# A latent-attention block: value-output parts loaded piece by piece, a query product over 128 rows, low parts of rotated weights on GpSimd

## The reference

```python
q_lat = rmsnorm(x @ q_a_w, q_a_norm_w)                       # 192 wide
q = (q_lat @ q_b_w).reshape(b, s, H, QKD).transpose(0, 2, 1, 3)
q_nope, q_pe = (q[..., :NOPE], q[..., NOPE:])                # 128, 64 (rotated)
kv = (rmsnorm(kv_lat, kv_a_norm_w) @ kv_b_w)...              # k_nope, v from 64
scores = (einsum(q_nope, k_nope) + einsum(q_pe, k_pe)) * QKD ** (-0.5)
idx_scores = einsum('bqn,bnqk->bqk', iw, relu(einsum('bqnd,bkd->bnqk', iq, ik)))
_, topk_idx = jax.lax.top_k(where(causal, idx_scores, -inf), 128)
attn = softmax(where(topk_mask & causal, scores, -inf))
out = einsum('bhqk,bhkd->bqhd', attn, v).reshape(b, s, H * VD) @ o_w
```

## Time and profile before

| | |
|---|---|
| median of 3 runs | 976.77 us (971.97 to 983.13) |
| profiled execution | 975.21 us, its span 973.4 us |
| TensorE busy | 841.5 us, 86% of the span |
| VectorE busy | 700.1 us, 72% |
| ScalarE busy | 597.6 us, 61% |
| GpSimd busy | 517.8 us, 53% |
| mean granted TensorE clock | 0.958 |
| DMA engines' mean busy share in queue 1 | 41.1% |

### The profile page before, as it was taken

The page is one execution under the profiler, slowest core; times in us unless marked ns, Lnnn a source line. Parts: engine busy times, 40 slices in busy tenths (PEclk is TensorE's granted clock), DMA queues, the critical chain, the costliest instruction groups (busy, mean ns, idle before and its releaser), DMA issues.

```text
span 973.4 us, 20180 instructions
## 1 busy us (share of the span) xinstructions
PE 841.5 (86%) x7496; PEld 503.0 (52%) x7496; DVE 700.1 (72%) x1589; ACT 597.6 (61%) x1324; POOL 517.8 (53%) x407
## 2 busy tenths in 40 slices
PE   5979989877775989888998998999999999929998
PEld 2535544443343555555555665666666666614443
DVE  5366677899999999999997777678777777710100
ACT  3657789875564878788877666567666666610000
POOL 2093378755442555455554777677877767510000
PEclk9989999987778999999999999999999999969999
DMA  7012111112232444444441677656676665670211
GB/s 234 23 44 85 57 48 51 60 42 82 80 87 65 126 127 125 115 120 128 127 124 55 117 132 115 129 113 120 122 135 131 116 117 107 129 229 1 65 44 44
DMA packets 168609, 96.65 MB, mean 99 GB/s; under 512 B 116545, under 2 KB 142529, under 8 KB 168513
## 3 DMA queue, kind: packets, MB, share of 16 engines
q1 hardware_dynamic: 168512, 95.37, 41.1%
HBM read 36.62 MB, written 6.29 MB: 44 GB/s over the span
## 4 chain that ended last, share of the span: by engine, by line
PE 49%; DVE 24%; issue 10%; POOL 7%; ACT 7%; DMA 2%; SPq 1%; POOLq 0%; DVEq 0%; ACTq 0%
PE psS L691 12%; PE psS L763 9%; DVE arena L1225 6%; PE psT L747 5%; DVE arena L1030 4%; ACT arena L794 4%; DVE m L1162 4%; PE psS L578 3%; DVE bias L1169 3%; PE psT L565 2%; PE psS L522 2%; PE psO L718 2%; POOL arena L1338 2%; POOL bias L1404 2%; PE psT L545 2%
## 5 line engine op out<-in xcount | busy, mean ns | idle before, releaser
L691 PE MATMUL psS<-keyT,arena 128*128 128x512 f16 (+3 forms) x1152 | 231.4, 329 | 29.3 <-issue 13.5
L979 ACT ACTIVATE arena<-arena,small 128x512 f32<-128x512 f32 (+7 forms) x256 | 198.2, 774 | 68.5 <-DVE small L1230 37.7
L794 ACT ACTIVATE arena<-psT 128x512 f16<-128x512 f32 (+4 forms) x360 | 172.2, 506 | 103.7 <-PE psT L747 45.9
L1030 DVE SCALAR_TENSOR_TENSOR arena<-psT,arena 128x512 f16<-128x512 f32 (+3 forms) x278 | 146.7, 547 | 96.6 <-ACT arena L794 96.0
L1225 DVE CUSTOM_DVE_ANT_0 arena<-psS,bias 128x512 f32<-128x512 f32 (+7 forms) x256 | 191.5, 748 | 0.1
L578 PE MATMUL psS<-ikT,big 128*128 128x512 f16 (+3 forms) x528 | 112.7, 362 | 30.7 <-DVE bias L1115 27.2
L691 PEld LDWEIGHTS psS<-keyT,arena 128*128 128x128 f16 x1152 | 91.4, 98 | 86.3 <-issue 18.8
L747 PE MATMUL psT<-ident,arena 128*128 128x128 f32 x736 | 115.8, 278 | 21.2 <-DVE arena L1030 18.0
L1404 POOL TENSOR_TENSOR bias<-arena,bias 128x768 f32<-128x768 f32 (+2 forms) x48 | 91.5, 1920 | 64.3 <-ACT arena L860 64.0
L747 PEld LDWEIGHTS psT<-ident,arena 128*128 128x128 f32 x736 | 84.6, 141 | 54.5 <-ACT arena L979 31.4
L578 PEld LDWEIGHTS psS<-ikT,big 128*128 128x128 f16 x528 | 51.6, 104 | 85.8 <-DVE bias L1115 34.0
(11 more groups left out here) (163 smaller groups left out, 1410.7 us busy)
## 6 DMA issues: line engine op xcount, KB each, us to landing
arena<-arena SPq DMA_DIRECT2D x192, 128.0 KB, 2.4
arena<-in_wiq SPq DMA_DIRECT2D x32, 256.0 KB, 2.7
arena<-in_ow SPq DMA_DIRECT2D x16, 512.0 KB, 3.5
arena<-in_qbT SPq DMA_DIRECT2D x16, 256.0 KB, 2.5
wvo_parts<-arena SPq DMA_DIRECT2D x16, 256.0 KB, 2.0
arena<-in_qpe SPq DMA_DIRECT2D x16, 128.0 KB, 2.9
arena<-in_x SPq DMA_DIRECT2D x8, 256.0 KB, 3.1
out<-arena SPq DMA_DIRECT2D x8, 256.0 KB, 2.1
```

Of the source, the lines that this page charges most:

```text
L691: last = mm(bank[:, k:k + w], Q[:, u % 2, h, a, q:q + P], keyT[:, b, h, k:k + w], start=(a, b) == (0, 0), stop=(a, b) == (1, 0))
L794: return nc.scalar.activation(dst, src, ACT.Copy, scale=scale)
L979: nc.scalar.activation(pr[:, g % 4, 0:kw], pr[:, g % 4, 0:kw], ACT.Exp, bias=shift[:, g % 4:g % 4 + 1], scale=-1.0, accum_out=rsum[:, unit ...
L1030: return v.scalar_tensor_tensor(out=dst, in0=src, scalar=scale, in1=hi, op0=ALU.mult, op1=ALU.subtract)
```

## The change

Three edits. (1) The 16 value-output parts are loaded one by one by SyncE in the second pass (`VO_AT` maps a step to a part), each behind a wait for the last reader of its place; TensorE waits for 16 loads in place of 5. (2) `qlT[64:128, 3]` is set to zero once (on GpSimd, semaphore `ql_zero`), and the last matmul of a query product takes all 128 rows of `w2s` and `qlT[:, 3]`. (3) The two low parts that come from `pe_s` move from VectorE to GpSimd (`pe_low`). [...] `qw_lo` counts two per pair now, and `pe_lo` two more; whoever waited for one waits for both.

```diff
@@ tables
+        VO_AT = {8 * u_ + s_: n_ for n_, u_, s_ in
+                 [(12, NP + 1, 6), (14, NP + 2, 6)]
+                 + [(n_, NP + 3 + 4 * (n_ % 4) + n_ // 4, 6) for n_ in range(12) if n_ % 4 < 3]
+                 + [(3, NU - 2, 2), (7, NU - 2, 4), (11, NU - 2, 6), (13, NU - 1, 0), (15, NU - 1, 2)]}
@@ SyncE
             def load_qw(p, u, first):
                 if not first:
-                    sp.wait_ge(qw_lo, 4 * p - 4)
+                    sp.wait_ge(qw_lo, 2 * p - 2)
+                    sp.wait_ge(pe_lo, 2 * p - 2)
...
+            def load_vo(n):
+
+                if n < 12:
+                    sp.wait_ge(qa_mm, NP + 4 * (n % 4) + 4)
+                else:
+                    sp.wait_ge(rot, 3 * (NP if n % 2 == 0 else NU))
+                sp.dma_start(wvo[n].rearrange("p s n -> p (s n)"), wvo_d[ds(n, 1)].rearrange("a p n -> (a p) n")).then_inc(ld_vo, 16)
+
...
                 if s == 7 and u < NP:
                     store_vo(u)
-
-
-            sp.wait_ge(qa_mm, NU)
-            for j, w_ in enumerate((w1hi, w1lo, w2s)):
-                sp.dma_start(w_[:].rearrange("p (a b) n -> p a (b n)", b=4),
-                             wvo_d[4 * j:4 * j + 4].rearrange("a p n -> p a n")).then_inc(ld_vo, 16)
-            sp.wait_ge(rot, 3 * NU)
-            for j, w_ in enumerate((cq, sq)):
-                sp.dma_start(w_[:].bitcast(F16).rearrange("p (a n) -> p a n", a=2),
-                             wvo_d[12 + 2 * j:14 + 2 * j].rearrange("a p n -> p a n")).then_inc(ld_vo, 16)
+                if g in VO_AT:
+                    load_vo(VO_AT[g])
@@ TensorE
-                mm(bank, w2s[0:64, p, ws], qlT[0:64, 3, cs], start=False, stop=True).then_inc(qp_mm if what == "R" else qa_mm, 1)
+                mm(bank, w2s[:, p, ws], qlT[:, 3, cs], start=False, stop=True).then_inc(qp_mm if what == "R" else qa_mm, 1)
...
-            pe.wait_ge(ld_vo, 80)
+            pe.wait_ge(ld_vo, 16 * NP)
@@ ScalarE
                 copy(w2s[:, n, 128:256], psT[u][:, 128:256], WQ_S).then_inc(qw_hi, 1)
+                act.wait_ge(qw_hi, 4 * n + 2)
+                copy(pe_s[:, u], pe_s[:, u], WQ_S).then_inc(pe_sc, 1)
@@ VectorE
-                dve.wait_ge(qw_hi, 4 * n + 2)
-                low(w1lo[:, n, 0:128], pe_s[:, u, 0, :], WQ_S, w1hi[:, n, 0:128]).then_inc(qw_lo, 1)
-                low(w2s[64:128, n, 0:128], pe_s[64:128, u, 1, :], WQ_S, w2s[64:128, n, 0:128]).then_inc(qw_lo, 1)
                 dve.wait_ge(qw_hi, 4 * n + 4)
@@ GpSimd
+            g.memset(qlT[:, 3, :], 0.0).then_inc(ql_zero, 1)
...
+            def pe_low(n):
+                pool.wait_ge(pe_sc, n + 1)
+                g.tensor_tensor(w1lo[:, n, 0:128], pe_s[:, n % 2, 0, :], w1hi[:, n, 0:128], ALU.subtract).then_inc(pe_lo, 1)
+                pool.wait_ge(pe_lo, 2 * n + 1)
+                g.tensor_tensor(w2s[64:128, n, 0:128], pe_s[64:128, n % 2, 1, :], w2s[64:128, n, 0:128],
+                                ALU.subtract).then_inc(pe_lo, 1)
+                pool.wait_ge(pe_lo, 2 * n + 2)
+
             for n in range(IH):
                 join(relu_a[:, n % 2], 7, 2 * IH + n, 2 * IH + n, 1 if n else 0)
+                pe_low(n)
```

More of the change, by code:

```diff
@@ L221, in block_kernel @@
         tk_max = sem("tk_max"); tk_rep = sem("tk_rep"); mask_done = sem("mask_done")
-        qn_done = sem("qn_done"); kc_done = sem("kc_done"); hw_done = sem("hw_done")
+        ql_zero = sem("ql_zero"); pe_sc = sem("pe_sc"); pe_lo = sem("pe_lo"); qn_done = sem("qn_done"); kc_done = sem("kc_done"); hw_done = sem("hw_done")
         tr_mm = sem("tr_mm"); tr_hi = sem("tr_hi"); tr_lo = sem("tr_lo")
@@ L337, in block_kernel @@
             MARK_STEPS.setdefault(i_ * 15 // 8, []).append(i_)
+        VO_AT = {8 * u_ + s_: n_ for n_, u_, s_ in
+                 [(12, NP + 1, 6), (14, NP + 2, 6)]
+                 + [(n_, NP + 3 + 4 * (n_ % 4) + n_ // 4, 6) for n_ in range(12) if n_ % 4 < 3]
+                 + [(3, NU - 2, 2), (7, NU - 2, 4), (11, NU - 2, 6), (13, NU - 1, 0), (15, NU - 1, 2)]}
+        assert len(VO_AT) == NP
         n_const = 8
@@ L445, in turn @@
                                        rows_of_turn(d)[:, 0:2 * nb * P]).then_inc(landed[d % 4], 16)
-            sp.wait_ge(qw_lo, 4 * NP)
+            def load_vo(n):
[4 more added lines that the diff above has]
+                sp.dma_start(wvo[n].rearrange("p s n -> p (s n)"), wvo_d[ds(n, 1)].rearrange("a p n -> (a p) n")).then_inc(ld_vo, 16)
+            sp.wait_ge(qw_lo, 2 * NP)
+            sp.wait_ge(pe_lo, 2 * NP)
             sp.wait_ge(acc_done, 4 * IH)
@@ L597, in qw_pair @@
                 if p >= 2:
-                    pe.wait_ge(qw_lo, 4 * p - 4)
+                    pe.wait_ge(qw_lo, 2 * p - 2)
                 for h in range(2):
@@ L639, in _ @@
             pe.wait_ge(tr_lo, TR_JOBS)
+            pe.wait_ge(ql_zero, 1)
             for n in range(IH):
@@ L650, in _ @@
                     else:
-                        pe.wait_ge(qw_lo, 4)
+                        pe.wait_ge(qw_lo, 2 * u + 2)
+                        pe.wait_ge(pe_lo, 2 * u + 2)
                     q_job(first_bank[what][:], what, u)
@@ L733, in _ @@
                 scores(g)
-            pe.wait_ge(qw_lo, 4 * NP)
+            pe.wait_ge(qw_lo, 2 * NP)
+            pe.wait_ge(pe_lo, 2 * NP)
             pe.wait_ge(raw_done, 2)
@@ L1152, in transposed_lo @@
                 dve.wait_ge(tr_hi, job + 1)
+                if job == 2:
+                    dve.wait_ge(ql_zero, 1)
                 low(dl[0:rows_, cs], tr_bank[job % 2][0:rows_, :], s, dh[0:rows_, cs]).then_inc(tr_lo, 1)
```

## The result

The changed kernel takes 928.5 us in the median (927.4 to 931.0, four runs), the kernel before on the same chip 974.4 us (969.9 to 983.1). The ratio is 0.952, with a 95% interval of 0.945 to 0.960. The forecast was 927 us; its terms did not come out as well as their sum. Of all runs reported here one execution, of experiment 3, was in a slower state of the chip; it is left out of that run's median.

What follows compares the result with a forecast made beforehand. VectorE was taken to bound the last indexer stage and first pass, TensorE the second pass, a load wait the end. A 19.0 + B 10 + C 20 - 1 for small items = 48 us off 975.2: 927, range 914 to 944.

Steps and rivals of the forecast that it cites:

- B: Last query product over 128 rows: 10 us gain, 7.5 in the second pass and 2.5 in the first; ends 3 and 17.
- C: Last indexer stage: two low parts moved from VectorE to GpSimd gain 20 us (25.4 less 5.4); ends 12 and 26.
- A: Kernel's end: value-output parts loaded inside the second pass gain 19.0 us (16.0 + 3.0); ends 16 and 21.
- the small items: Zeroing at GpSimd's start costs nothing; issue and traffic of 16 part loads in the second pass cost 1 us, ends 0 and 8.
- Rival 2: Kernel's end: loading the parts in the second pass gains 10 us, 936 in all; chance 0.07.
- rival 4: Second pass: part loads delay transposes and placing, 58 us come back, 984 in all; chance 0.03.
- rival 3: Query products: the 128-row form gains nothing, 937 in all; chance 0.06.
- the 0.41 us per job: TensorE time that full rows save per query product, 0.52 + 0.32 - 0.43; 28 jobs in the second pass, 11.5 us.
- The discount for the heads: Second pass: waits for the query tile at unit heads give time back, so two thirds of 11.5 taken: 7.5 us.
- two deductions: Last indexer stage: 3 us for TensorE's slow clock and 2.4 for late pair loads, off 25.4 us.
- Rival 1: Last indexer stage: two rounds of three run at 6.5 us, stage about 97, gain 11, 936 in all; chance 0.15.
- rival 5: Last indexer stage: a wait makes GpSimd's low parts late every round, stage gains nothing, 947 in all; chance 0.04.

Runs made afterwards that it cites:

- experiment 3: The kernel before with only the 128-row last query product and the zeroing of the rows it adds; 969.6 us, ratio 0.995.
- experiment 6: The changed kernel with the next unit's latent half placed ahead of the unit's first transpose (step 0 instead of 1); 913.6 us, ratio 0.938.
- 9: The changed kernel with the latent half placed at step 0 and the low parts back on VectorE; 943.6 us.
- 10: The kernel before with only the latent placing moved to step 0 from step 1; 957.8 us, ratio 0.985.
- experiment 8: The kernel before with GpSimd's additions of tile 7's index sums in the third indexer stage cut to 8 columns instead of 1024; 961.3 us, stage 94.8.
- 7: The changed kernel with the latent half placed at step 0 and the last query product over 64 rows again; 917.1 us.
- 1: The changed kernel with the value-output parts loaded behind the second pass again, in five transfers; 949.5 us.

## Why the prediction was right, and where its steps were not

The total (48 us forecast, 47.8 in the profiled executions) is right partly by luck: B came 5.5 us short, and C's stage gave 6.4 us more than forecast, a loss in the second pass that no step had took 3.8 of these back, and A and the small items gave 2.8 more.

**A: 19.0 forecast, 20.8 measured.** The 16.0 us wait went, the first tile took 10.36 us for 13.38 (these are the 3.0 of the sum) at a granted clock of 1.00, where it had been 0.78 before and 0.50 in the tile's first 3 us, and the last transposes were covered, as argued. Another 1.7 us came from the third tile (12.22 to 10.54 us), which the sum doesn't hold; they are not A's. Its wait of 2.0 us for VectorE is in every profile, and behind it the tile took 12.22 us in six of the twelve and 10.53 or 10.54 in the other six. With the loads in the pass it was fast in four and slow in two (experiments 6 and 9, end 97.3 us); with the loads behind it, fast in two (3 and 10) and slow in four. What decides it no run here shows. Rival 2 (A of 10 us, 936 in all) is out. A alone gave the end of 95.5 us again, and the loads in the pass cost nothing in two pairs (329.8 and 329.9; 329.2 and 329.1). That settles rival 4, and the term for small items, where I took 1 us. (Most of the loads took about 1.1 us of issue, where I had reckoned up to 0.9, and landed 3.7 us after it in the median, where I had read 2.7; neither reached the path.)

**B: 10 forecast (7.5 in the second pass), 4.5 measured.** The mechanism was right, full rows bring the steps to 0.22 us (715.04, 715.26, 715.48 in experiment 6), and rival 3 (B of nothing, 937 in all) is out. The step that failed is the 0.41 us per job: it was read from the starts of the weight loads. The load of a full-row product starts 0.21 us ahead of it (566.61 against 566.82 us before; 715.05 against 715.26 in experiment 6). The load of the 64-row product, and that of the product behind it, start only 0.01 us ahead of theirs (567.13 against 567.14, 567.45 against 567.46). So the 0.52 us step began from a load that had been early, and 0.21 of the 0.41 us is this lead. The starts of the products themselves are 0.64 us apart over two steps, against 0.44: 0.20 us. The discount for the heads was a third; 4.5 of 5.6 is a fifth. The heads' waits bear it out: B adds 1.0 to 1.3 us to them (10.9 to 12.2 us without C, 15.0 to 16.0 and 14.8 to 15.9 with it). The other 3.8 of the 5 us in the first two tables of waits are C's. (With the placing moved B gave 5.4 us with C, and 3.9 without C in a pair that differs in A too, so a single pair is good to about a microsecond.) The trace of before had the product rows too. The first pass gave nothing: 0.1 us between the main pair, and between -2.5 (longer with B) and +0.7 in five pairs that differ in B, against the 2.5 that I took. In that stretch VectorE is busy 204 of 218 us, and the 3.2 to 7.5 us by which TensorE is less busy in these pairs go into its idle.

**C: 20 forecast, 26.4 in its stage, 22.6 net.** The period of 5.15 us was forecast, 5.14 came, with 82.1 us for the stage. My two deductions, 3 us for the clock and 2.4 for late pair loads, were both for things that didn't happen: VectorE waited for nothing in the whole stage, TensorE's idles between the rounds were 1.70 us at most, and its clock 0.98. The slow spells are gone, and with them the idles of 2.3 to 3.6 us that had stood before them; I had argued that way and then not trusted it. (Such an idle was not always followed by a slow spell: before, the groups behind 3.55 us at 293.43 and 3.52 us at 300.38 us took 1.31 us.) The 5.3 us that I reckoned from VectorE's accumulation to the low parts' end kept nobody waiting. Rival 1, rounds of 6.5 us, is out, and so is rival 5. That the lows were slowed by GpSimd's addition is shown by experiment 8. The lows that stay on VectorE, with one input in PSUM, average 0.28 and 0.30 us with GpSimd busy 63 of 82 us. Without the two deductions C had 25.4 us. The stage gave them, and 1.0 more (VectorE's own idle there fell from 3.3 to 1.5 us).

The step that was missing is C's price in the second pass: the prediction put it at nothing without a word, and it is 3.5 to 3.9 us in three comparisons, all as wait for the placing at the heads (3.6 to 4.1 us). With the placing early and 128 rows 0.4 us of it is left; with 64 rows it may be 2.1 us, in a pair that differs in A too (experiments 7 and 10). In one unit, from 161 us into the pass on, I laid the traces of experiments 3 and 1 side by side: shifted by the 1.3 us that they were apart at its start, the engines' instructions and the end of the placing's issue agree within 0.1 us, and the head is released 0.5 us later with C. Why the transfers land later, when C changes nothing that runs then, stays open, since no experiment took it apart.

**The sum, by the parts alone:** 20.8 + 4.5 + (26.4 - 3.8) = 47.9. The three singles, by their medians, are 19.6 (A), 4.8 (B) and 23.0 (C): 47.4 against 45.8 together. To within the spread of the runs the parts add up.

The sign that the prediction named, a second pass of about 328 us, came (329.1) for another reason than the one given, since its 7.5 was really 4.5 and a loss of 3.8. A sum that fits confirms no term.

## What to carry to other kernels

Price a matmul form by the starts of matmuls on both sides of it, not by the starts of weight loads, which here ran ahead by one product and made a stall of 0.20 us look like 0.41. Where a profile shows an idle "issue" at the head of every unit, look at what the DMA queue issues just ahead of it, and whether an item that is ready stands behind one that waits: here moving two ready transfers past a waiting transpose gave about 15 us, more than the 128-row product did, for one moved statement. And before moving work off a busy engine, count what its neighbour's long instruction adds to short ones; half of what C won was that.

## What the runs showed of the hardware

- One 64-row product among 128-row ones costs 0.20 us more than a full one of the same 512 columns (0.64 against 0.44 us over two steps, in 28 jobs of a pass), though it has half the rows.
- VectorE subtractions with both inputs in SBUF, 0.28 us alone, took 2.31 us beside GpSimd's 128x1024 addition of 2.35 us in the earlier trace rows, and ended within 0.14 us of it. GpSimd's own addition was not slower for it: 2361 ns on average before, 2359 with the subtractions gone.
- TensorE took 1.31 us for each group of six products behind 14 idles of 0.62 and 1.70 us, at a granted clock of 0.98 over the stage. In the kernel before, with idles of up to 3.6 us, it was 0.81. Behind one and the same idle of 2.0 us, ahead of the third output tile, 48 products took 10.5 us in six profiles and 12.2 in six.
- Adding 16 loads of 256 KB to a pass whose DMA share was 0.64 raised that to 0.70 and its traffic from 118 to 132 GB/s, and cost no time (329.8 and 329.9 us without and with them, in the kernel before).
